# A router's gate products placed between the 512-column products of the shared expert

## The reference

```python
x = x + layernorm(attention(layernorm(x)))
xf = layernorm(x).reshape(n, 256)
logits = xf @ gate_w.T                       # 16 experts
scores = sigmoid(logits)                     # + gate_bias, best 2 of 4 groups, best 4 experts
cw = weights of the chosen experts, normalised, times 2.5
y = sum over chosen experts: (silu(xf @ Wg.T) * (xf @ Wu.T) * cw) @ Wd.T
shared = silu(xf @ Ws_g.T) * (xf @ Ws_u.T) @ Ws_d.T
x = x + layernorm(xf + y + shared)
```

## Time and profile before

| what | us |
|---|---|
| runs of the kernel | 1142.09, 1718.08, 1135.75 (median 1142.09) |
| the profiled execution, its own time | 1133.88 |
| its span in the profile | 1132.1 |

### The profile page before, as it was taken

The page is one execution under the profiler, slowest core; times in us unless marked ns, Lnnn a source line. Parts: engine busy times, 40 slices in busy tenths (PEclk is TensorE's granted clock), DMA queues, the critical chain, the costliest instruction groups (busy, mean ns, idle before and its releaser), DMA issues.

```text
span 1132.1 us, 22264 instructions
## 1 busy us (share of the span) xinstructions
PE 884.2 (78%) x7190; PEld 657.4 (58%) x7190; DVE 673.3 (59%) x1943; ACT 463.4 (41%) x788; POOL 447.0 (39%) x422
## 2 busy tenths in 40 slices
PE   2448878899897987978886888598799978899660
PEld 1335545566565565655564555487687866788450
DVE  5364647577678677576666675555533355572843
ACT  1104434543543543542543555245444544455220
POOL 1330302203525416403511414357557754566450
PEclk9767979788899798797887998899999998899885
DMA  3485556433644444432667212455556697757833
GB/s 131 118 179 136 147 130 158 118 82 83 155 119 110 114 120 132 105 106 73 185 179 255 79 59 78 131 173 188 161 167 215 206 353 257 254 174 245 318 149 130
DMA packets 108654, 177.51 MB, mean 157 GB/s; under 512 B 15232, under 2 KB 79744, under 8 KB 108288
## 3 DMA queue, kind: packets, MB, share of 16 engines
q1 hardware_dynamic: 93952, 135.45, 43.1%
q0 software_dynamic: 14592, 40.65, 9.5%
HBM read 92.35 MB, written 83.17 MB: 155 GB/s over the span
## 4 chain that ended last, share of the span: by engine, by line
PE 39%; DVE 16%; issue 11%; SPq 10%; POOL 10%; DMA 9%; ACT 5%; POOLq 0%; DVEq 0%; ACTq 0%
PE ring L1260 6%; POOL expert_rows L666 6%; PE ring L1386 5%; PE ring L1194 4%; DMA q_st<-mrow 4%; PE ring L1231 4%; PE ring L1246 3%; SPq L523 3%; PE ring L1196 3%; PE ring L1195 3%; DVE nmax L744 2%; ACT prob L1124 2%; DMA xg<-sorted_rows 2%; PE ring L1407 2%; SPq L569 2%
## 5 line engine op out<-in xcount | busy, mean ns | idle before, releaser
L744 DVE TENSOR_REDUCE nmax<-ring 128x2 f32<-128x1024 f32 (+3 forms) x256 | 201.4, 818 | 81.6 <-PE ring L1237 79.3
L1124 ACT ACTIVATE prob<-ring 128x1024 f32<-128x1024 f32 (+1 forms) x192 | 165.3, 879 | 190.4 <-PE ring L1251 189.1
L666 POOL DMA_INDIRECT expert_rows<-ys,dest x176 | 180.7, 1027 | 120.2 <-ACT ys L1080 58.6
L1386 PE MATMUL ring<-we,xh 128*128 x704 | 174.7, 393 | 0.0
L1246 PE MATMUL ring<-q_st,k_st 50*128 50x384 f32 (+3 forms) x512 | 109.1, 441 | 83.9 <-DMA q_st<-mrow 53.8
L658 POOL DMA_INDIRECT sorted_rows<-xr,idx_all x128 | 128.4, 1003 | 94.6 <-DVE xr L903 60.8
L1386 PEld LDWEIGHTS ring<-we,xh 128*128 128x128 f32 x704 | 132.9, 199 | 15.8
L1231 PE MATMUL ring<-k_st,q_st 48*128 48x512 f32 (+3 forms) x512 | 112.9, 447 | 24.9 <-ACT prob L1124 20.9
L963 DVE SCALAR_TENSOR_TENSOR sl<-sl,got,ring 128x128 f32<-128x128 f32 x176 | 53.1, 343 | 126.5 <-ACT sl L1176 122.4
L636 POOL TENSOR_TENSOR rot<-rot 128x512 f32<-128x512 f32 x16 | 20.3, 1271 | 261.7 <-DVE rot L736 261.7
L1246 PEld LDWEIGHTS ring<-q_st,k_st 50*128 50x128 f32 x512 | 55.6, 209 | 111.6 <-issue 74.1
(11 more groups left out here) (189 smaller groups left out, 1616.9 us busy)
## 6 DMA issues: line engine op xcount, KB each, us to landing
xg<-sorted_rows SPq DMA_DIRECT2D x176, 134.0 KB
parts<-part SPq DMA_DIRECT2D x32, 512.0 KB, 5.9
ykt<-expert_rows SPq DMA_DIRECT2D x8, 2048.0 KB, 10.4
k_st<-parts SPq DMA_DIRECT2D x64, 128.0 KB, 3.7
q_st<-parts SPq DMA_DIRECT2D x64, 128.0 KB, 3.5
sorted_rows<-zeros SPq DMA_DIRECT2D x3, 2144.0 KB, 10.2
sorted_rows<-zeros SPq DMA_DIRECT2D x48, 134.0 KB, 2.6
we<-w_exp SPq DMA_DIRECT2D x1, 6144.0 KB, 19.9
```

The source lines that it names most:

```text
L666: pool.indirect_dma_start(out=yk, out_offset=bass.IndirectOffsetOnAxis(ap=dest[:, j % 8, b:b + 1], axis=0), in_=ys[:, j % NYS, b, :], in_o ...
L744: dve.tensor_reduce(nmax[:, Q % 2, :, pp, qb], slot[:, :, col:col + (qb + 1) * P], AX.X, ALU.max, negate=True).then_inc(s_max, 1)
L1124: act_e.activation(prob[:, u % 2, 2 * half:2 * half + 2, 0:width], slot[:, :, 0:width], ACT.Exp, scale=SCALE).then_inc(s_exp, 1)
L1386: last = pe.matmul(G_BANK[j % 2][:, b, :], xh[:, j % 2, b, k, :], we_cols[:, bass.ds(columns[j, b] + k * D, D)], start=(k == 0), stop=(k = ...
```

## The change

On PE the second GU step of a sequence (u = 1) and the LG step become one function. It issues the same 12 products of 512 columns in the same order, and after each of them takes the next gate products from a generator: two after the first of each triple, one after each of the other two. The gate products keep their order, operands and destination. The semaphores are counted up at the products that complete the same results: s_gu after the sixth and after the twelfth long product, s_logit after the last gate product, which now comes directly behind the twelfth. The wait for M_BANK's previous user moves from ahead of LG to ahead of the first of the 28 products. PLAN, and with it DVE, ACT, POOL and SP, stays as it was.

```diff
--- before.py
+++ after.py
@@ -1261,15 +1261,30 @@
                                          prob[:, u % 2, j, col:col + T - kb * P], start=(kb == 0), stop=(m == UNITS - 1))
                 last.then_inc(s_av, 1)
 
-            def logits_unit(s):
+            def logit_products():
+
                 for t in range(NT):
                     tok = slice(t * P, (t + 1) * P)
-                    dst = M_BANK[:, t * 2 * E:(t + 1) * 2 * E]
                     for k in range(KD):
-                        pe.matmul(dst, h_lo[:, k, tok], w_gate[:, k, :, :].rearrange("p c e -> p (c e)"), start=(k == 0), stop=False)
-                        last = pe.matmul(dst, h_hi[:, k, tok], w_gate[:, k, :, :].rearrange("p c e -> p (c e)"), start=False,
-                                         stop=k == KD - 1)
-                last.then_inc(s_logit, 1)
+                        cols = w_gate[:, k, :, :].rearrange("p c e -> p (c e)")
+                        for half, rows_h in enumerate((h_lo, h_hi)):
+                            yield pe.matmul(M_BANK[:, t * 2 * E:(t + 1) * 2 * E], rows_h[:, k, tok], cols,
+                                            start=k == 0 and half == 0, stop=k == KD - 1 and half == 1)
+
+            def gate_up_and_logits(slot, u):
+
+                logits = logit_products()
+                last_logit = None
+                for gu in range(2):
+                    for k in range(KD):
+                        w_h, w_l = weights((C_SG, C_SU)[gu], k, D, u * P, P)
+                        for n, (left, right) in enumerate(((w_l, h_hi), (w_h, h_lo), (w_h, h_hi))):
+                            last = pe.matmul(slot[:, gu, :], left, right[:, k, :], start=k == 0 and n == 0,
+                                             stop=k == KD - 1 and n == 2)
+                            for _ in range(2 if n == 0 else 1):
+                                last_logit = next(logits, None) or last_logit
+                    last.then_inc(s_gu, 1)
+                last_logit.then_inc(s_logit, 1)
 
             def count_unit(s):
                 pe.matmul(M_BANK[:, 0:NT * E], below_b[:, :], r_m[:, :], start=True, stop=False, skip_group_check=True)
@@ -1296,7 +1311,7 @@
                 kind, n = st[0], st[1]
                 before = RING_BEFORE.get(st) or M_BEFORE.get(st)
                 slot = ring[RING_SLOT[st]] if st in RING_SLOT else None
-                if before is not None:
+                if before is not None and kind != "LG":
                     pe.wait_ge(*free_of(before))
                 if kind == "XT":
                     pe.wait_ge(s_xn, NT * (n + 1))
@@ -1343,11 +1358,12 @@
                 elif kind == "HT":
                     pe.wait_ge(s_xn2, NT * (n + 1))
                     transpose_rows(slot, xr[:, n % 2, :, :], s_hT)
-                elif kind == "LG":
-                    pe.wait_ge(s_htlo, KD * (n + 1))
-                    logits_unit(n)
                 elif kind == "GU":
                     pe.wait_ge(s_htlo, KD * (n + 1))
+                    if st[2] == 1:
+                        pe.wait_ge(*free_of(M_BEFORE["LG", n]))
+                        gate_up_and_logits(slot, 1)
+                        continue
                     for gu in range(2):
                         channel_product(slot, gu, h_hi, h_lo, (C_SG, C_SU)[gu], D, st[2] * P, gu == 1).then_inc(s_gu, 1)
                 elif kind == "SD":
```

## The result

The changed kernel took 1148.87 us (median of 16 runs, 1143.52 to 1151.72) against 1139.88 us for the kernel before, timed beside it. The ratio is 1.0079, with a 95% interval of 1.0054 to 1.0105: about 9 us slower, where I had forecast 1.1 us. The ratios leave out executions more than 1.5% above the fastest of the same kernel, which the medians still hold, so the two can differ. Two later timings of the same pair gave 1.0039 (1.0009 to 1.0069) and 1.0068 (1.0034 to 1.0103). The mean of the three is 1.0062, 7.1 us on 1141. The time lies in the range of 1124 to 1153 and within the 2% that I called no change, but all three intervals lie above 1, and the loss is larger than the forecast.

What follows compares the result with a forecast made beforehand. No engine is full, so the chain of waits bounds the kernel, with the logits' sum on it in seven sequences. 0 + 4.6 - 3.5 = +1.1 us; from the 1137.2 average, 1138 us was predicted, range 1124 to 1153.

Steps and rivals of the forecast that it cites:

- PE's own time: Second half plus gate on PE: 4.50 us before and after the change, so a cost of 0.
- bounds of 1.3: PE's gate products: 1.3 us gained a sequence if loads hide entirely, 1.3 us lost if each waits for a whole load.
- rival 2: Gate's weight loads hide behind the long products: 1.3 us earlier in seven sequences, -9.1, 1129 us; chance 0.1.
- rival 3: Each alternation costs a load, 0.19 instead of 0.111 us per gate product; with the multiply's delay +13.7, 1151 us; chance 0.15.
- The sign that I had named for the two: On PE, a gate-to-512-column distance other than 0.111 us would show that loads hide or that alternation costs a load.
- The order of the results: DVE's logit sum stands behind the late multiply: 0.65 us, at most 0.73, later in seven sequences, +4.6 us.
- One mark: Sign that the forecast is right: ACT idles 2.1 instead of 1.48 us before the sigmoid r_sc.
- silu at nothing: ACT's silu of the second half comes 0.89 us later, hidden in ACT's idling before r_sc, at no cost.
- The clock: Half-clock stretches behind the gate: two of five shorten (-4.6), even chance that sequence 5 loses its luck (+1.1): -3.5 us.
- Rival 1: Clock stays up behind the gate, since the stretch before its fall is denser: about -8.6, 1129 us; chance 0.2.

Runs made afterwards that it cites:

- e1: The changed kernel, but VectorE sums the logits before it multiplies the second half; 1137.62 us, ratio to before 0.9952.
- r6: The kernel of e1 timed again: the changed kernel with the logits summed before the second multiply; 1138.31 us, ratio to before 0.9969.
- r9: The kernel of e1 timed a third time: the changed kernel with the logits summed before the second multiply; 1144.34 us, ratio to before 0.9998.
- e2: The kernel before, gate products still as a run, but VectorE's second multiply also waits for the logits; 1148.39 us, ratio to before 1.0047.
- r7: The kernel of e2 timed again: the kernel before with VectorE's second multiply waiting for the logits; 1147.20 us, ratio to before 1.0073.
- e4: Against the kernel before: the gate's run between the second half's two sets of six long products, logits summed before the second multiply; 1136.72 us, ratio 0.9947.
- e5: e4 plus a one-column exponential on ACT right behind the first a_hi, pulling the table load ahead; 1134.15 us, ratio to before 0.9954.
- e8: e2 plus five reductions over 128x512 on VectorE ahead of the logits' sum; 1167.31 us, ratio to before 1.0210.

## Why the prediction was wrong

- **PE's own time: 0.** Right: +0.07 us in sequence 0, inside the bounds of 1.3. Loads are started one ahead in the mixed order too, so rival 2 (loads hide) falls, and rival 3 (each alternation costs a load) falls with it: a pair of a long and a gate product takes 0.34 us, 0.227 + 0.111. The sign that I had named for the two, a distance from a gate to a long product other than 0.111 us, was badly chosen: 0.03 us is recorded behind a single gate product, and the pair still costs its 0.34. The same record misled me on the price of rival 2, whose 0.03 us (220.43 to 220.46) is no cost of a product either. e1, r6 and r9 agree by time: they are not slower than the kernel before.
- **The order of the results: +0.65 us, at most 0.73, in seven sequences, 4.6 us.** Right in mechanism, and the measured 0.68 to 0.72 us lies at its upper end: 4.9 us. r_lg stands directly behind the multiply, PE's wait is 2.59 us where about 2.6 was foretold, in sequences 0 to 5, and 1.51 instead of 0.88 in sequence 6. One mark was off: ACT idles 1.39 us before r_sc, not 2.1. I had put silu at nothing, which holds, but forgot that a later silu also takes idle time out of that bracket. It is 0.81 us later; I had said 0.89 for eight gate products, and only seven stand ahead of the sixth long one (0.78). For PE it changes nothing.
- **The clock: -3.5 us.** This is the step that failed. I priced a short instead of a long half-clock stretch at PE's 2.3 us from its restart to the first product of the down projection (SD), and let that run to the end of the span. The stretches did change as guessed, but two things stand between SD and the end. The first is that the way on from SD is not set by PE alone: after SD comes DVE's z (L1063), and DVE's part doesn't follow PE's clock (the 16 z of the kernel before take 672 to 692 ns each). Sequence 2 shows it. Before, PE restarts at 389.76, SD starts at 398.31 and z at 402.03. After:

```profile
390.05 0.50 PE L1231 MATMUL ring<-k_st,q_st 48*128 48x512 f32 x2 [2.58 <-ACT prob L1124]
...
396.33 0.39 PE L1194 MATMUL ring<-w_hi,a_lo 128*128 128x256 f32 x1
...
401.11 1.28 DVE L1063 TENSOR_TENSOR z<-ring,xr 128x512 f32<-128x512 f32 x2
```

PE's way to SD fell from 8.55 to 6.28 us, by 2.3; the way to z from 12.27 to 11.06, by 1.2. Over the sequences, the ways to z of 1, 2 and 3 gave 3.5 us in this profile, and 5 and 6, with longer half-clock stretches than before, took 3.0 of it back. Summed over the seven sequences, from the timeline and the granted clock of each profile (the last two columns are us at half clock, first from the second half's first product to z, then from z to the next sequence's first product of that kind):

| sums, us | restart to SD | restart to z | half clock to z | half clock behind z |
|---|---|---|---|---|
| before | 51.7 | 73.4 | 54.6 | 81.9 |
| changed, three profiles | 49.1, 49.5, 49.7 | 73.0, 72.1, 72.5 | 47.8, 47.8, 47.7 | 95.6, 92.2, 95.6 |
| e2, r7 (run, late) | 52.6, 52.9 | 75.8, 76.3 | 64.9, 64.9 | 95.6, 95.6 |
| e1, r9 (mixed, early) | 46.8, 45.6 | 70.1, 68.3 | 34.1, 34.1 | 95.6, 116.1 |
| e4 | 42.8 | 67.6 | 20.5 | 105.8 |
| e5 | 38.3 | 65.7 | 0.0 | 133.1 |

For the changed kernel it is -2.3 us at SD and only -0.9 at z in the mean. That alone doesn't settle the term, because there is one profile of the kernel before, and it is of a fast execution (1133.88 us): against e2 and r7, with their run of gate products and an equally late restart, the mixed order is 3.5 us shorter at z. But in the ends nothing of it is seen: 1.0062 mixed against 1.0060 as a run.

The second thing is behind z. e5 shows it best: it has no half clock at all up to z, and its z come 16.5 us earlier in sum than before, 8.8 of them from the restart. From z to the next sequence's first product it then takes 380.5 instead of 364.3 us, 16.2 us more, with 51 us more at half clock. The changed kernel's first profile takes 370.8 us there, 6.5 more than before, with 14 more at half clock. So a half-clock stretch that goes at this place can come back at a later one, and a term for the clock can't be priced at the place of the change. How much comes back in the mean isn't shown: these are single executions, and this part differs by 6 us among the changed kernel's own three profiles (370.8, 365.3, 371.4). Not all of it seems to: over the executions of each timing the granted clock averages 0.864 to 0.866 in the changed kernel and 0.861 to 0.864 in the kernel before. Where that little is lost on the way to the end stays open. Without the clock term the sum would have been 0 + 4.6, and with the measured delay 4.9.
- **What stays open.** 4.9 us direct against 7.1 us timed, and in the first timing 9.0 us (6.2 to 12.0). e8 rules out that a delay of that size is amplified, and the other two timings (4.5 and 7.8 us) lie around the direct value and above it. The same pair of kernels gave middles 0.4% apart in three timings, as did e1 and its repeats (0.9952 to 0.9998). The medians of the three timings differ by 9.0, 0.1 and 5.5 us (1148.87 against 1139.88, 1143.48 against 1143.36, 1146.68 against 1141.21), 4.9 in the mean. So 2 us are at the edge of what was measured, and I have no cause for them.
- **Rival 1, the clock stays up.** It falls: in sequence 0 the half level comes later but is as long as before, 10.24 us, all stretches at this place still hold 47.8 of 54.6 us, and the kernel is not faster. One reading under it was off: I had the clock fall 0.2 us into PE's idling, but by the bracket of 1.99 us at 225.81 the idling began at 223.82, 0.5 us ahead of the fall.

e1, e4 and e5 were each faster than the kernel before in their first timing, by about 0.5%; e1 didn't keep it in the repeats. e4 and e5 were timed once.

## What to carry to other kernels

When instructions of one engine are mixed, both results of the mixture come at its end, and the engine that consumes them in a fixed order delays whichever it takes second by the whole of the first; look at the consumer's order, and take first what the chain of waits needs. A delay on a path without slack is worth itself times its count (here 0.72 x 7), and a cheap test is to put more of it in. Measure it by where the waiting engine goes on, counted from a fixed instruction: the length of a wait also shrinks when the work ahead of it ends later. A gain by TensorE's clock is not to be read on TensorE, nor at one place: follow it to the next engine that waits, and look at the half-clock time behind.

## What the runs showed of the hardware that was not expected

- ACT's table load waited for its activation's semaphore though it uses none of the data behind it: in e4 it starts at 224.49 after 1.13 us of idling; with a one-column exponential ahead of it (e5) it starts at 222.79, 0.02 us behind a_hi. A switch costs 1.28 us here and the activation follows 0.01 us later.
- The fall of the clock moved with the products, but not in any way that I can compute. In sequence 0 it came at 224.3 before, after 0.5 us of idling, and at 226.88 in the changed kernel, after PE had hardly run for 2.6 us (0.16 us busy). The Trainium skill ("TensorE: Matmul & The Clock Gate", "Why this matters for your kernels") names idle gaps as what takes the clock down. The runs agree in part: the time at half clock up to z goes with PE's wait, from none at 0.51 us (e5) over 20.5 at 1.53 (e4) and 54.6 at 1.99 (before) to 64.9 at 2.58 (e2, r7). But at the same wait as in e2 and r7 the changed kernel has less of it, 47.8 at 2.59, so the wait alone doesn't set it; and in sequence 2 of the changed kernel the fall came at 390.72, after PE had gone on at 390.05.
- Half clock that goes at one place can come back at another: e5 has none up to z and 133.1 us behind it, where the kernel before has 54.6 and 81.9.
